# Three row normalisations moved from VectorE to ScalarE, with their bias formed on GpSimd

## The reference

```python
def _layernorm(x, axis=-1, eps=1e-05):
    m = jnp.mean(x, axis=axis, keepdims=True)
    v = jnp.var(x, axis=axis, keepdims=True)
    return (x - m) / jnp.sqrt(v + eps)
...
x = x + _layernorm(_L0_attn_ref(_layernorm(x, axis=-1), ...), axis=-1)
x = x + _layernorm(_L0_ffn_ref(_layernorm(x, axis=-1), ...), axis=-1)
```

```python
scores = jnp.where(mask, -jnp.inf, jnp.einsum('bhid,bhjd->bhij', q, k) * scale)
att_dot = jnp.einsum('bhij,bhjv->bhiv', jax.nn.softmax(scores, axis=-1), v)
sq = jax.nn.elu(q) + 1.0
att_mem = sq @ M / (sq @ jnp.swapaxes(Z, -2, -1))
M_new = M + jnp.einsum('bhld,bhlv->bhdv', jax.nn.elu(k) + 1.0, v)
att = gate * att_mem + (1.0 - gate) * att_dot
out = att.reshape(B, LSEG, H * DV) @ Wo
```

## Time and profile before

| | us |
|---|---|
| median of 3 runs | 1267.12 (1265.22 to 1268.21) |
| the profiled execution | 1260.22 |
| its span, first to last instruction | 1258.4 |
| PE busy | 1070.4 (85%) |
| DVE busy | 846.4 (67%) |
| ACT busy | 611.5 (49%) |
| POOL busy | 584.2 (46%) |
| L760, the normalisations, on DVE | 68.7 busy (x100), 36.6 idle before |
| ScalarE's scale-and-bias form, L680 | 26.2 busy (x48), 592 ns each |

### The profile page before, as it was taken

How to read it: one execution, slowest core, us unless ns; L and a number is a source line. 1 busy time by engine, 2 the same in 40 slices (tenths; PEclk the granted TensorE clock), 3 DMA queues, 4 the chain that set the end, 5 groups by cost and what they waited for, 6 DMA issues and landing times.

```text
span 1258.4 us, 20680 instructions
## 1 busy us (share of the span) xinstructions
PE 1070.4 (85%) x7172; PEld 739.7 (59%) x7172; DVE 846.4 (67%) x1492; ACT 611.5 (49%) x1291; POOL 584.2 (46%) x715
## 2 busy tenths in 40 slices
PE   2898989897898898878888888888989879999972
PEld 1476767664766675656666666666767666433331
DVE  3868686866687868657777787878686752434375
ACT  3554544544354544434445454545445552566663
POOL 2145454553454545444545454545454551323266
PEclk9999999988999999979999999999999988999995
DMA  6100000000000000000000000000000010300014
GB/s 154 30 10 9 10 9 10 10 13 8 10 9 9 9 10 10 10 11 9 10 8 11 10 10 9 10 10 9 9 2 9 2 28 1 142 0 0 1 34 101
DMA packets 14954, 24.02 MB, mean 19 GB/s; under 512 B 5376, under 2 KB 7168, under 8 KB 14336
## 3 DMA queue, kind: packets, MB, share of 16 engines
q1 hardware_dynamic: 14848, 22.63, 6.3%
HBM read 13.97 MB, written 8.65 MB: 18 GB/s over the span
## 4 chain that ended last, share of the span: by engine, by line
PE 46%; DVE 33%; issue 10%; ACT 6%; POOL 2%; DMA 1%; DVEq 0%; SPq 0%; POOLq 0%; ACTq 0%
PE ps L1111 11%; PE ps L1216 10%; DVE arena L816 8%; PE ps L1329 6%; PE ps L1169 4%; DVE arena L913 3%; PE ps L1342 3%; DVE arena L847 3%; DVE arena L760 3%; ACT arena L576 2%; PE ps L1174 2%; DVE arena L830 2%; DVE arena L826 2%; PE ps L1156 2%; DVE arena L865 2%
## 5 line engine op out<-in xcount | busy, mean ns | idle before, releaser
L1111 PE MATMUL ps<-arena 128*128 128x512 f16 x1152 | 272.5, 388 | 7.2 <-DVE arena L792 5.2
L576 ACT ACTIVATE arena<-ps,arena 128x128 f32<-128x128 f32 x512 | 139.3, 383 | 224.5 <-DVE arena L837 223.9
L816 DVE STREAM_TRANSPOSE arena<-ps 128x1024 f32<-128x1024 f32 x96 | 190.2, 1983 | 40.6 <-PE ps L1111 40.5
L1111 PEld LDWEIGHTS ps<-arena 128*128 128x128 f16 x1152 | 113.5, 100 | 131.8 <-issue 17.6
L420 POOL TENSOR_TENSOR arena<-arena 128x256 f32<-128x256 f32 x128 | 93.0, 727 | 151.8 <-DVE arena L847 151.6
L1169 PE MATMUL ps<-arena 128*128 128x65 f32 x1024 | 136.0, 277 | 16.3 <-DVE arena L847 15.1
L1169 PEld LDWEIGHTS ps<-arena 128*128 128x128 f32 x1024 | 132.3, 197 | 29.8 <-issue 21.4
L404 POOL TENSOR_TENSOR arena<-arena 128x512 f32<-128x512 f32 x64 | 81.3, 1270 | 119.5 <-ACT arena L569 119.4
L1216 PE MATMUL ps<-arena 128*128 128x256 f32 x544 | 122.0, 382 | 0.3 <-ACT arena L588 0.3
L390 POOL TENSOR_TENSOR arena<-arena 128x2 f32<-128x2 f32 x50 | 9.8, 197 | 235.6 <-DVE arena L756 235.6
L752 DVE BATCH_NORM_STATS2 arena<-arena 128x6 f32<-128x256 f32 x100 | 36.7, 409 | 111.6 <-ACT arena L594 97.4
(11 more groups left out here) (109 smaller groups left out, 1845.8 us busy)
## 6 DMA issues: line engine op xcount, KB each, us to landing
x_rows<-arena SPq DMA_DIRECT2D x17, 256.0 KB, 2.0
arena<-in_L_attn_x_dram SPq DMA_DIRECT2D x64, 64.0 KB
arena<-x_rows SPq DMA_DIRECT2D x4, 1024.0 KB, 8.2
out_dram<-arena SPq DMA_DIRECT2D x32, 128.0 KB, 2.9
arena<-in_L_attn_Wq_dram SPq DMA_DIRECT2D x1, 1024.0 KB, 13.8
arena<-in_L_attn_Wk_dram SPq DMA_DIRECT2D x1, 1024.0 KB, 19.3
arena<-in_L_attn_Wv_dram SPq DMA_DIRECT2D x1, 1024.0 KB, 22.7
arena<-in_L_attn_Wo_dram SPq DMA_DIRECT2D x8, 128.0 KB, 10.5
```

Of the source, the lines that this page charges most:

```text
L576: last = act.activation(Pr[:, par, j, :], s_bank[:, par, j * P:(j + 1) * P], ACT.Exp, bias=negm[:, par, j:j + 1])
L816: dve.transpose(dst[:, d0:d0 + 32, :], bank.rearrange("p w (d c) -> p d w c", c=C)).then_inc(x_free, 1)
L1111: last = pe.matmul(bank[:, w, :], xc[:, lx, k, w * P:(w + 1) * P], W16[lw][:, k, i, :], start=(n == 0), stop=(n == 5))
```

## The change

The two instructions of a normalisation, `(x - mean) * rs` with `rs` = (var + eps)^(-1/2), become two ScalarE activations with the function Identity, `rs * x + nb`, with `nb` = -mean * rs. `rs` and `nb` are one number for each partition, handed over by pointer. GpSimd forms `nb` in `deviation` with two more instructions over 128x2: mean times -1 beside the addition of eps, and times `rs` behind the power. The counts on the semaphores go from 2 to 4 for each use. On ScalarE the calls stand at hand-picked places: `n_norm` behind `take_y`, `y_norm` behind `exp_k` of group 2, `x2_norm` behind `take_p` of group 2. VectorE keeps the sums. In the start, two `n_norm` stand around the first `take_n`; in the second block `y_norm` stands behind `layer4(0, 0)` and `x2_norm` behind `stage(1)`.

```diff
-                def deviation(rs, mv, stat, done, n):
+                def deviation(rs, nb, mv, stat, done, n):
                     pool.wait_ge(stat, n * 4)
                     pool.tensor_tensor(rs, mv[:, :, 1], eps, ALU.add).then_inc(done, 1)
-                    pool.wait_ge(done, n * 2 - 1)
+                    pool.tensor_tensor(nb, mv[:, :, 0], minus, ALU.mult).then_inc(done, 1)
+                    pool.wait_ge(done, n * 4 - 2)
                     pool.tensor_tensor(rs, rs, mhalf, ALU.pow).then_inc(done, 1)
+                    pool.wait_ge(done, n * 4 - 1)
+                    pool.tensor_tensor(nb, nb, rs, ALU.mult).then_inc(done, 1)
...
+                def norm_rows(dst, src, rs, nb):
+                    for w in range(2):
+                        last = act.activation(dst[:, w * D:(w + 1) * D], src[:, w * D:(w + 1) * D], ACT.Identity,
+                                              scale=rs[:, w:w + 1], bias=nb[:, w:w + 1])
+                    return last
+                def n_norm(r, n):
+                    act.wait_ge(n_rstd, n * 4)
+                    norm_rows(nrow, xrow[r], n_rs, n_nb).then_inc(xn_done, 1)
+                def y_norm(bp, s):
+                    m = bp * NSEG + (s + 1)
+                    act.wait_ge(y_rstd, m * 4)
+                    norm_rows(row, row, r_rs, r_nb).then_inc(yn_done, 1)
+                def x2_norm(bp, s):
+                    m = bp * NSEG + (s + 1)
+                    act.wait_ge(x2_rstd, m * 4)
+                    norm_rows(row, xrow[(s + 3) % 4], r_rs, r_nb).then_inc(x2n_done, 1)
...
+                n_norm(0, 1)
                 take_n((0, 0), 0, 1)
+                n_norm(1, 2)
                 weights(0)
...
                     take_y(t_job(bp, s, "Y"))
+                    if ahead:
+                        n_norm((s + 2) % 4, bp * NSEG + (s + 3))
                     take_q(bp, s, 2)
                     exp_k(bp, s, 2)
+                    y_norm(bp, s)
                     if ahead:
                         take_n(t_job(bp, s, "N"), s % 2, bp * NSEG + (s + 3))
                     probs(bp, s, 2)
                     take_p(bp, s, 2)
+                    x2_norm(bp, s)
                     take_q(bp, s, 3)
...
                 layer4(0, 0)
+                y_norm(PAIRS - 1, NSEG)
                 stage(1)
+                x2_norm(PAIRS - 1, NSEG)
                 take_f(t_job(PAIRS - 1, NSEG, "F"), NT - 1)
...
-                def normalise(dst, src, mv, rs):
-                    for w in range(2):
-                        last = dve.tensor_scalar(dst[:, w * D:(w + 1) * D], src[:, w * D:(w + 1) * D],
-                                                 mv[:, w, 0:1], rs[:, w:w + 1], ALU.subtract, ALU.mult)
-                    return last
...
                 n_stats(0, 64, 1)
-                n_norm(0, 1)
+                dve.wait_ge(xn_done, 1)
                 n_stats(1, 64, 2)
                 split((0, 0), 0, 1)
-                n_norm(1, 2)
                 low_weights(0)
...
-                    if ahead:
-                        n_norm((s + 2) % 4, bp * NSEG + (s + 3))
                     y_stats(bp, s)
                     take_q(bp, s, 2)
                     divide(bp, s, 1, 0)
-                    y_norm(bp, s)
                     if not last:
                         take_x(bp, s, 3)
...
                     x2_stats(bp, s)
-                    x2_norm(bp, s)
                     take_q(bp, s, 3)
```

More of the change, by code:

```diff
@@ L132, in infini_block_kernel @@
         n_rs, r_rs = alloc(2), alloc(2)
-        eps, mhalf = alloc(2), alloc(2)
+        n_nb, r_nb = alloc(2), alloc(2)
+        eps, mhalf, minus = alloc(2), alloc(2), alloc(2)
         spare = alloc(1)
@@ L374, in _ @@
                 pool.memset(mhalf, -0.5).then_inc(consts, 1)
-                pool.wait_ge(consts, 6)
+                pool.memset(minus, -1.0).then_inc(consts, 1)
+                pool.wait_ge(consts, 7)
                 for m in (identf, identb):
@@ L385, in _ @@
                 pool.memset(v_pos[0].rearrange("p (u e) -> p u e", u=UNITS)[:, :, DK:DV1], 1.0).then_inc(init, 1)
-                def deviation(rs, mv, stat, done, n):
+                def deviation(rs, nb, mv, stat, done, n):
                     pool.wait_ge(stat, n * 4)
                     pool.tensor_tensor(rs, mv[:, :, 1], eps, ALU.add).then_inc(done, 1)
-                    pool.wait_ge(done, n * 2 - 1)
+                    pool.tensor_tensor(nb, mv[:, :, 0], minus, ALU.mult).then_inc(done, 1)
+                    pool.wait_ge(done, n * 4 - 2)
                     pool.tensor_tensor(rs, rs, mhalf, ALU.pow).then_inc(done, 1)
+                    pool.wait_ge(done, n * 4 - 1)
+                    pool.tensor_tensor(nb, nb, rs, ALU.mult).then_inc(done, 1)
                 for t in range(2):
-                    deviation(n_rs, n_mv, n_stat, n_rstd, t + 1)
+                    deviation(n_rs, n_nb, n_mv, n_stat, n_rstd, t + 1)
                 pool.wait_ge(w_lo, 6)
@@ L427, in y_dev @@
                 def y_dev(bp, s):
-                    deviation(r_rs, r_mv, y_stat, y_rstd, bp * NSEG + (s + 1))
+                    deviation(r_rs, r_nb, r_mv, y_stat, y_rstd, bp * NSEG + (s + 1))
                 def residual(bp, s):
@@ L437, in x2_dev @@
                 def x2_dev(bp, s):
-                    deviation(r_rs, r_mv, x2_stat, x2_rstd, bp * NSEG + (s + 1))
+                    deviation(r_rs, r_nb, r_mv, x2_stat, x2_rstd, bp * NSEG + (s + 1))
                 def step(bp, s, ahead=True):
@@ L445, in step @@
                     if ahead:
-                        deviation(n_rs, n_mv, n_stat, n_rstd, bp * NSEG + (s + 3))
+                        deviation(n_rs, n_nb, n_mv, n_stat, n_rstd, bp * NSEG + (s + 3))
                     y_dev(bp, s)
@@ L766, in n_stats @@
                     rows_stats(n_st, n_mv, xrow[r], n_stat, n)
-                def n_norm(r, n):
-                    dve.wait_ge(n_rstd, n * 2)
-                    normalise(nrow, xrow[r], n_mv, n_rs).then_inc(xn_done, 1)
                 def split(job, par, n):
@@ L866, in remember @@
                         last.then_inc(t_free[b], 1)
-                def y_norm(bp, s):
-                    m = bp * NSEG + (s + 1)
-                    dve.wait_ge(y_rstd, m * 2)
-                    normalise(row, row, r_mv, r_rs).then_inc(yn_done, 1)
-                def x2_norm(bp, s):
-                    m = bp * NSEG + (s + 1)
-                    dve.wait_ge(x2_rstd, m * 2)
-                    normalise(row, xrow[(s + 3) % 4], r_mv, r_rs).then_inc(x2n_done, 1)
                 def y_stats(bp, s):
@@ L1051, in _ @@
                 y_stats(PAIRS - 1, NSEG)
-                y_norm(PAIRS - 1, NSEG)
                 update(0, 0)
                 x2_stats(PAIRS - 1, NSEG)
-                x2_norm(PAIRS - 1, NSEG)
                 seq_sums(PAIRS - 1, NSEG)
@@ L1077, in _ @@
             def _(pe):
-                pe.wait_ge(consts, 9)
+                pe.wait_ge(consts, 10)
                 def turn_rows(job, src, ready, n):
```

## The result

The changed kernel took 1280.84 us, the median of 4 runs (1276.85 to 1282.91), against 1266.17 (1263.08 to 1268.21, 4 runs) for the kernel before on the same chip: ratio 1.0114, 95% interval 1.0080 to 1.0148. It is slower by 1.1%, and the forecast was 1279.7 on 1267.1.

A forecast was written before the change was run, and what follows sets the result against it. No single engine bounds the kernel; late hand-overs along the chain do. 11 x 0.83 + 0.2 + 1.8 - 0.2 = 10.9, plus ends 0.2 and 1.5, gives 12.6; 1272.8 profiled, 1279.7 median against 1267.1, range 1271 to 1288.

The forecast's parts named there:

- The price of Identity: ScalarE's scale-and-bias activation: 0.50 us start to start, 0.59 alone, read from the second block; low bound 0.26.
- not slower: Rival: ScalarE overlaps contiguous Identity rows at 0.26 us each, total 1266.5, within the noise; chance 0.05.
- n, +1.00: Between take_y and take_q: two activations join the chain, while VectorE's freed time falls into idle; +1.00 us a step.
- y, -1.75: VectorE goes from divide straight to take_x, ScalarE's y work hidden; -1.75 us a step.
- x2, +1.58: From x2's sums to VectorE's next take_q: GpSimd's release, two activations, then ScalarE's take_q in sequence; +1.58 us a step.
- last steps of three pairs: Steps with the short-copy memory update: +0.2 us in the first pair, partly absorbed by a TensorE wait, +0.9 in two others.
- very last step: Final step of the last pair: ScalarE is late already and y's gain pays for x2; 0.
- second block: Later y on ScalarE 0.7, GpSimd's deviation 0.45 and longer activations 0.36 delay the x2 normalisation; +1.5 us.
- The start's +0.2: At the kernel's start, GpSimd's +0.45 and ScalarE's n come before the weights, whose DMA ends the wait; +0.2 us.
- add 6.9: The median of the runs lies 6.9 us above the profiled execution, so 1272.8 becomes 1279.7.
- Slack behind takes part of it: Rival: VectorE's waits after the second take_q absorb the delay in half of eleven steps; 1275.1; chance 0.16.
- TensorE's clock: Rival: a new gap of 2 us each step drops TensorE's clock, 11 x 1.0 us more; 1290; chance 0.12.

The follow-up runs named there:

- e1: The changed kernel with only the n normalisation put back on VectorE; 1265.81 us, ratio 0.9993 to the kernel before.
- e2: The changed kernel with n_norm still on ScalarE but ahead of take_y instead of behind it; 1268.19 us, ratio 1.0014 to the kernel before.
- f1: The kernel before with only n moved to ScalarE, behind take_y; y and x2 on VectorE; 1288.58 us, ratio 1.0189.
- e7: The kernel before with only y moved to ScalarE, n and x2 on VectorE; 1235.23 us, ratio 0.9743.
- e8: The kernel before with only x2 moved to ScalarE, ahead of take_q of group 3; 1304.86 us, ratio 1.0287.
- f2: e8 plus six useless matmuls in TensorE's gap ahead of its wait for split; 1292.77 us, ratio 1.0212 to the kernel before.
- e5: The changed kernel run again, unaltered, on a second chip; 1281.63 us, ratio 1.0112 to the kernel before.
- e6: The changed kernel plus six repeated matmuls filling TensorE's gap ahead of job F; 1279.83 us, ratio 1.0093 to the kernel before.
- f3: The changed kernel with n_norm ahead of take_y and x2_norm behind exp_k of group 3; 1217.14 us, ratio 0.9614 to the kernel before.
- f4: The changed kernel with n_norm as one 512-column activation instead of two of 256, so n's numbers are partly wrong; 1281.45 us, one run.

## Why the prediction was right

In the regular steps, the first three of a pair, the reasons held, term by term.

- **The price of Identity**: 588 ns and 0.49 to 0.50 apart, as read off the second block. The low bound of 0.26, on which "not slower" rested, is out.
- **n, +1.00**: measured +0.98 (e1, e2, f1). The reason, idle time on VectorE that pays nothing and a queue place ahead of an awaited instruction, is shown by e2, where the place alone is changed.
- **y, -1.75**: measured -1.73 (e7).
- **x2, +1.58**: measured +1.53 (e8), +1.58 (f2: 16.81). VectorE idle 4.26, ended by ScalarE's Exp, forecast "nearly 4.3"; GpSimd's release and take_q's share came within 0.03.
- **The step**: 62.68 against 62.7, in first and second steps of a pair. TensorE's gap before job F 2.12 for "about 2".

The sum again, each term as measured in steps without a stretch at half clock:

| term | forecast | measured |
|---|---|---|
| 11 regular steps with n | +9.1 | +9.5 |
| last steps of three pairs | +2.0 | +3.8 |
| third step of the last pair | -0.2 | -0.3 |
| very last step | 0 | +1.0 |
| second block | +1.5 | +0.9 |
| sum, without the start | 12.4 | 14.9 |

The measured ones are differences of the intervals above; of the last steps of pairs, 1 to 2 (+0.98) and 2 to 3 (+0.30) count. The 9.5 holds 1.0 that no term of the forecast has, the wait in the third steps (last section). The very last step is 12.31 against 11.27 in these two profiles, and 12.10 in e5's.

The step that failed is "ScalarE is late already and y's gain pays for x2: 0". In the very last step VectorE waited 0.51 for ScalarE before; after, the x2 wait is the full one, and y's gain went nowhere: 2 to 3 is 12.34 there with x2 alone on ScalarE (e8) and 12.31 with y too, although y alone brings it to 10.43 (e7). VectorE's last `take_q` before and after:

```profile
1028.78 0.69 DVE L825 SCALAR_TENSOR_TENSOR arena<-ps,arena 128x512 f32<-128x512 f32 x1 [0.51 <-ACT arena L554]
```

```profile
1049.77 0.69 DVE L847 SCALAR_TENSOR_TENSOR arena<-ps,arena 128x512 f32<-128x512 f32 x1 [4.26 <-ACT arena L581]
```

The last steps of pairs were mis-sized too. They lose 0.30 in the interval 2 to 3, where the others gain 0.20: y alone gives 1.34 there (e7) instead of 1.73, and x2 costs 1.65 (e8) instead of 1.53. For y, the first copy of the short memory update takes 1.01 us where it took 0.61:

```profile
273.31 0.61 DVE L784 COPY arena<-arena 64x260 f32<-64x260 f32 x2
```

```profile
536.74 1.01 DVE L807 COPY arena<-arena 64x260 f32<-64x260 f32 x2
```

The forecast let the first pair's delay vanish in a wait of 0.69 us for TensorE. That wait came behind a stretch at half clock (0.61 over 274 to 282), so it belongs to one execution, and the table counts the place without it. In the second block the deviation didn't hold x2 as thought. GpSimd was done at 1100.34, and ScalarE was busy with a layer of its own until the activations began at 1100.96; from the y sums (ended 1090.55) to job F it is 11.54 us against 10.60 before, +0.94. ScalarE and TensorE there:

```profile
1100.96 1.08 ACT L528 ACTIVATE arena<-arena 128x256 f32<-128x256 f32 x2
```

```profile
1102.09 0.66 PE L1094 MATMUL ps<-arena 128*128 128x128 f32 x4 [1.76 <-ACT arena L528]
```

The start's +0.2 could not be measured: the first `take_q` of group 1 lies anywhere between 59.2 and 62.7 us in the profiles, whichever kernel ran.

One part of the forecast was not argued well. The profile before lay 6.9 us under the median, the profile after 1.1 above its own, mostly by stretches at half clock. To add 6.9 as it stood took a median execution of the changed kernel to have as many of them as one before. It came out so, 14.7 between the medians for 14.9 of counted places, but no row said it would, and in the kernels with one part alone it didn't. That part of the hit was luck. The sum itself came out 2.5 us too small, mostly by the last steps of pairs (+3.8 for +2.0) and the very last step (+1.0 for 0).

The rivals. *Slack behind takes part of it*: in first and second steps it didn't. *Not slower*: its price didn't occur. *TensorE's clock*: the mechanism is real, and it is the older gap that costs time. Behind the new gap before job F the clock did fall, in six of the fifteen steps ahead of the last in the profile after, but filling it (e6) won 2 us at most. With the old gap, which `split` ends, e8 and f1 lose 12 us and 10 us beyond their places, and f2, which fills it, gets 9.5 back. The change as a whole mostly escaped, since y on ScalarE brings that gap to 1.25; in the third steps it is 1.6, and there the clock fell behind it in two of three (the 15.68 and 16.34 above). "Against: the gap before `split` shrinks in exchange" was the right sentence. Why the chance of a drop grows with the gap and also, at an equal 2.2 us, differs from step to step stays open.

Additivity is the blind spot: the sum treats n, y and x2 as three independent numbers. As places they nearly are: to 0.05 us in first and second steps, but not in the third steps (0.34 more, with n and y together) nor in the very last (0.8). As times they aren't: alone they moved the median by +24, -33 and +36 us, which sum to 27, and all three together gave 14.7. Their places alone are about +14, -26 and +25, which sum to 13, near what the three together gave.

## What to carry to other kernels

An idle share doesn't say where an engine is free. Put moved work into an idle time of the new queue and behind what others wait for: here the same 100 instructions on the same engine cost +1.1% in one order and gave -4.1% in the other. Before a wait is put into an in-order queue, read what stands behind it and whether it could have been done meanwhile. And where one part of a change shortens a gap of the matmul engine, it may carry a gain that the other parts then spend; measure the parts alone as well as together.

## What the hardware showed that was not expected

- The granted clock fell to 0.50, for some 3 to 7 us, at TensorE gaps of 2.2 us too, and not each time. Of the eleven regular steps that have n, the clock fell at the gap ahead of the memory update in all eleven with 2.9 us (f1), in eight with 2.2 (e8), in three with 2.2 (the kernel before), and in none with 0.5 (e7) or 0.9 (f2).
- In the third step of each looped pair VectorE waits 0.48 us between its reciprocal and the multiplication behind it, in every kernel that has n and y both on ScalarE (after, e2 to e6, f3, f4), and in none of the others (before, e1, e7, e8, f1, f2). It costs 0.34 us of the interval 2 to 3 each time and, in the kernel after, widens TensorE's next gap from 1.25 to 1.6:

```profile
469.58 0.69 DVE L869 TENSOR_TENSOR arena<-ps,arena 128x512 f32<-128x512 f32 x1 [0.48 <-DVE arena L866]
```

  The profile puts the wait down to VectorE itself; what ended it wasn't found.
- Twelve matmul instructions that do nothing of use, put into a gap, made e8 faster by some 9.5 us of 1305.
